# The opening of a recommendation tower on one core: forty gathers in fours that wait for their landing, and a second group of indices spread by products

## What is computed

```python
e = jnp.stack([tbl_0[ids[:, 0]], ..., tbl_39[ids[:, 39]]], axis=1)
z = jnp.einsum('bpd,pde,bpe->bp', e[:, iidx, :], bilinear_matrices, e[:, jidx, :])
h = jnp.concatenate([z, dense_ctx], axis=1)
h = jnp.maximum(h @ W_top1 + b_top1, 0.0)
h = jnp.maximum(h @ W_top2 + b_top2, 0.0)
y = h @ W_top3
```

## Time and profile before

| what | value |
| --- | --- |
| median of 3 runs | 728.96 us (727.7 to 730.28) |
| the profiled execution, its own time | 728.67 us |
| its span, first to last instruction | 726.9 us |
| PE busy | 693.9 us (95%) |
| DVE busy | 597.1 us (82%) |
| POOL busy | 522.2 us (72%) |
| ACT busy | 197.1 us (27%) |
| granted TensorE clock, mean | 0.998 of full speed |
| gathers issued | 416, mean 986 ns |
| pauses | 208, mean 537 ns |

### The profile page before, as it was taken

One profiled execution on the slowest core, in us unless ns is written; L12 is line 12 of the kernel. 1 busy time (PEld: TensorE's weight loads), 2 busy tenths in 40 slices (PEclk: granted clock), 3 DMA queues, 4 the chain that ended last, 5 costly groups with the idle time before them and its releaser, 6 DMA issues.

```text
span 726.9 us, 15700 instructions
## 1 busy us (share of the span) xinstructions
PE 693.9 (95%) x6512; PEld 215.8 (30%) x6512; DVE 597.1 (82%) x608; ACT 197.1 (27%) x309; POOL 522.2 (72%) x631
## 2 busy tenths in 40 slices
PE   2767999999999999999999999999999999999998
PEld 2233333332332232322332232322332222222232
DVE  7989999999986989979876998979967878787800
ACT  3344411422052113043142103143143012213102
POOL 7888888888887888888887888888888887830000
PEclk9999999999999999999999999999999999999999
DMA  4555351222004020000004020000001000000000
GB/s 126 111 89 86 60 99 40 58 52 43 12 12 71 12 40 13 11 12 13 12 12 71 12 35 18 11 12 12 12 12 16 12 12 12 12 8 1 1 1 1
DMA packets 62692, 22.77 MB, mean 31 GB/s; under 512 B 46287, under 2 KB 61805, under 8 KB 62621
## 3 DMA queue, kind: packets, MB, share of 16 engines
q1 hardware_dynamic: 49277, 14.86, 8.8%
q0 software_dynamic: 13312, 6.84, 8.2%
q10 hardware_dynamic: 32, 0.07, 0.1%
HBM read 21.65 MB, written 0.07 MB: 30 GB/s over the span
## 4 chain that ended last, share of the span: by engine, by line
PE 89%; DVE 5%; ACT 4%; DMA 1%; issue 1%; ACTq 0%; DVEq 0%
PE U L940 28%; PE bank_z L965 26%; PE misc L992 14%; PE misc L891 10%; PE U L992 4%; PE U L949 3%; DVE ones L792 3%; PE U L914 3%; ACT x_T L645 1%; DMA idx_wide<-idx_rows 1%; DVE prod L828 1%; ACT x_twin L663 1%; PE bank_z L973 0%; DVE tabs L779 0%; ACT x_twin L666 0%
## 5 line engine op out<-in xcount | busy, mean ns | idle before, releaser
L589 POOL DMA_INDIRECT rows<-in_tbl,idx x416 | 410.2, 986 | 121.3 <-issue 63.5
L828 DVE TENSOR_TENSOR prod<-U,x_T 128x1024 f32<-128x1024 f32 x280 | 329.5, 1216 | 56.5 <-PE U L940 53.7
L965 PE MATMUL bank_z<-prod,select 128*32 128x512 f32 x1600 | 213.1, 604 | 0.7 <-ACT z L625 0.7
L940 PE MATMUL U<-x_T,W 32*128 32x512 f32 x1184 | 187.0, 640 | 7.4 <-ACT x_T L636 3.6
L792 DVE TENSOR_SCALAR ones<-idx_wide,row_of 125x2048 bf16<-125x2048 f16 x140 | 119.0, 872 | 7.0 <-ACT idx_wide L691 3.4
L891 PE MATMUL misc<-ones,tabs 125*32 125x512 bf16 x1680 | 108.4, 388 | 7.3 <-DVE ones L792 5.3
L597 POOL MEMSET pause<- 128x448 uint8 x208 | 111.7, 537 | 0.1
L828 DVE TENSOR_TENSOR prod<-U,x_look 128x1024 f32<-128x1024 f32 x80 | 94.3, 1218 | 21.0 <-PE U L940 18.5
L992 PE MATMUL misc<-z,W 128*32 128x512 f32 x728 | 92.0, 592 | 0.0
L940 PEld LDWEIGHTS U<-x_T,W 32*128 32x128 f32 x1184 | 57.8, 183 | 102.9 <-issue 49.4
L636 ACT ACTIVATE x_T<-U 32x512 f32<-32x512 f32 (+2 forms) x48 | 28.3, 591 | 188.8 <-PE U L914 115.0
(11 more groups left out here) (67 smaller groups left out, 284.1 us busy)
## 6 DMA issues: line engine op xcount, KB each, us to landing
rows<-in_tbl,idx POOLq DMA_INDIRECT x416
idx_wide<-idx_rows SPq DMA_DIRECT2D x13, 500.0 KB
W<-in_W_top SPq DMA_DIRECT2D x100, 8.0 KB
W<-_L_rec_bilinear_matrices SPq DMA_DIRECT2D x72, 16.0 KB, 3.2
prod<-in_tbl SPq DMA_DIRECT2D x4, 156.2 KB
W<-in_W_top SPq DMA_DIRECT2D x35, 2.0 KB
W<-_L_rec_bilinear_matrices SPq DMA_DIRECT2D x4, 128.0 KB
W<-in_W_top SPq DMA_DIRECT2D x1, 512.0 KB
```

The lines of the kernel that those rows point to most:

```text
L589: nc.gpsimd.indirect_dma_start(out=rows[:, n % R_SLOTS, t, f, :], out_offset=None, in_=tables[field][:, :], in_offset=bass.IndirectOffsetO ...
L828: last = nc.vector.tensor_tensor(to[:, :, m * N:(m + n) * N].rearrange("p r (m n) -> p r m n", m=n), U[:, at:at + 2, m * N:(m + n) * N].re ...
L940: last = nc.tensor.matmul(U[:, at + r % 2, m * N:(m + 1) * N], W[row, at_W:at_W + P], x_of(o, a)[row, :], start=True, stop=True, skip_grou ...
L965: last = nc.tensor.matmul(bank_z[r * DIM:(r + 1) * DIM, 0:N], sel, prod[:, (2 * g + r // 2) % P_SLOTS, r % 2, m * N:(m + 1) * N], start=(k ...
```

## The change

Two parts.

1. **Gathers.** The first 40 gathers are issued in fours without the pause; after each four, GpSimd waits until all that were begun on the slot of the last one have landed. From the 41st on, the pairs with pauses stand as before.
2. **Opening.** VectorE converts the first block's indices of all 16 looked-up fields first (4 casts for 1), and clears `rows[:, 1:5]` after that. TensorE spreads the indices of group 1 by 16 more products, and ScalarE copies them into `idx_wide[1]`; the read of `idx_wide` for block 0, group 1 leaves SyncE's list. Group 0's table is split between the one-hots (after two of them, not after five), group 1's follows, and the turned indices for memory come four looks later. ScalarE's clearing of `dense`, VectorE's splits of group 3 and ScalarE's `keep_look(0, 1)` move as well.

The constants `HELD, HELD_BURST = 40, 4` stand beside `BURST = 2`. The diff:

```diff
--- before.py
+++ after.py
@@ -322,6 +322,7 @@
 
 
 BURST = 2
+HELD, HELD_BURST = 40, 4
 
 
 U_SLOTS = 3
@@ -525,7 +526,6 @@
             for f in GROUPS[3]:
                 load_tab(sp, 3, f)
             sp.wait_ge(idx_stored, 16)
-            load_wide(0, 1)
             load_W(2)
             for f in GROUPS[2]:
                 load_tab(sp, 2, f)
@@ -592,7 +592,10 @@
                                 ap=idx[:, OFF[o] // P + t, field:field + 1], axis=0),
                         ).then_inc(gathered[n % R_SLOTS], 16)
                         begun[n % R_SLOTS] += 1
-                        if sum(begun) % BURST == 0:
+                        if sum(begun) <= HELD:
+                            if sum(begun) % HELD_BURST == 0:
+                                pool.wait_ge(gathered[n % R_SLOTS], 16 * begun[n % R_SLOTS])
+                        elif sum(begun) % BURST == 0:
                             pauses += 1
                             nc.gpsimd.memset(pause[:], 0).then_inc(paused, 1)
                             pool.wait_ge(paused, pauses)
@@ -690,22 +693,24 @@
             act.wait_ge(wide_full, 1)
             nc.scalar.activation(idx_wide[0][:], U[0:KP, 2:2 + CF, :], ACT.Copy).then_inc(wide_made, 1)
 
-            nc.scalar.activation(dense[:].rearrange("p t r d -> p t (r d)"),
-                                 ident[:].unsqueeze(1).to_broadcast([P, SUBS, P]), ACT.Copy, scale=0.0
-                                 ).then_inc(dense_zeroed, 1)
             split_hi(0)
             split_mid(0)
+            act.wait_ge(wide_full, 2)
+            nc.scalar.activation(idx_wide[1][:], U[0:KP, 2:2 + CF, :], ACT.Copy).then_inc(wide_made, 1)
+            split_hi(1)
+            split_mid(1)
             act.wait_ge(idx_T_full, 1)
             nc.scalar.activation(idx_T, U[0:NL, 0:BATCH // NB, :].rearrange("p b n -> p (b n)"), ACT.Copy
                                  ).then_inc(idx_T_made, 1)
             act.wait_ge(idx_T_made, 1)
             act.dma_start(idx_rows[:, :], idx_T).then_inc(idx_stored, 16)
-            split_hi(1)
-            split_mid(1)
+            nc.scalar.activation(dense[:].rearrange("p t r d -> p t (r d)"),
+                                 ident[:].unsqueeze(1).to_broadcast([P, SUBS, P]), ACT.Copy, scale=0.0
+                                 ).then_inc(dense_zeroed, 1)
             keep_look(0, 0)
             split_hi(3)
+            keep_look(0, 1)
             split_mid(3)
-            keep_look(0, 1)
             split_hi(2)
             for g in range(-2, G + 1):
                 if g == 4:
@@ -748,9 +753,6 @@
             nc.vector.tensor_copy(ident_h[:], ident[:]).then_inc(ident_h_made, 1)
             dve.wait_ge(row_of_made, 1)
             nc.vector.tensor_copy(row_of[:], row_of_i[:]).then_inc(row_of_f_made, 1)
-            nc.vector.memset(rows[:, 1:5], 0.0).then_inc(rows_zeroed, 1)
-
-
             beside = [(LOOKED.index(f), f, n) for f, n in ((36, 4), (0, 1), (24, 1), (2, 2), (16, 1), (9, 1), (34, 1),
                                                            (23, 1), (28, 1), (22, 1), (30, 1), (27, 1))]
 
@@ -760,7 +762,8 @@
                 return last
 
             dve.wait_ge(ids_loaded, 16)
-            to_half(0, ROWS[0] // P, beside[:1]).then_inc(idx_h_made, 1)
+            to_half(0, ROWS[0] // P, beside[:4]).then_inc(idx_h_made, 1)
+            nc.vector.memset(rows[:, 1:5], 0.0).then_inc(rows_zeroed, 1)
             for a in range(0, CHUNKS, 2):
                 zero = nc.vector.memset(W[:, w_col(a, a):w_col(a, a) + P], 0.0)
             zero.then_inc(W_zeroed, 1)
@@ -783,10 +786,10 @@
                 N, fs = ROWS[o], GROUPS[q]
                 n, job = LOOK_PART[(o, q, k)], LOOK_ORDER.index((o, q))
                 if k == 0:
-                    if job == 0:
-                        dve.wait_ge(wide_made, 1)
+                    if job < 2:
+                        dve.wait_ge(wide_made, job + 1)
                     else:
-                        dve.wait_ge(wide_landed[job % 2], 16 * ((job + 1) // 2))
+                        dve.wait_ge(wide_landed[job % 2], 16 * (job // 2))
                 if n >= ONES:
                     dve.wait_ge(ones_used, n - ONES + 1)
                 nc.vector.tensor_scalar(ones[:, n % ONES, 0:len(fs), 0:N], idx_wide[job % 2][:, 0:len(fs), 0:N],
@@ -833,32 +836,31 @@
                 last.then_inc(multiplied, 1)
 
             dve.wait_ge(row_of_f_made, 1)
-            for k in range(ONES):
+            for k in range(2):
                 one_hot(0, 0, k)
+            split_rest(0)
+            one_hot(0, 0, 2)
+            split_low(0)
+            one_hot(0, 0, 3)
+            split_rest(1)
             dve.wait_ge(ids_rest_loaded, 16)
-            to_half(ROWS[0] // P, BATCH // P, beside[:1])
-            to_half(0, BATCH // P, beside[1:]).then_inc(idx_h_rest_made, 1)
-            split_rest(0)
-            split_low(0)
-            for k in range(ONES, KC):
+            to_half(ROWS[0] // P, BATCH // P, beside[:4])
+            to_half(0, BATCH // P, beside[4:]).then_inc(idx_h_rest_made, 1)
+            for k in range(4, KC):
                 one_hot(0, 0, k)
-                if k == ONES + 1:
-                    split_rest(1)
-                if k == ONES + 3:
+                if k == 5:
                     split_low(1)
             nc.vector.memset(select[:], 0.0).then_inc(select_zeroed, 1)
             nc.vector.memset(rows[:, 5:7], 0.0).then_inc(rows_zeroed, 1)
             for k in range(KC):
                 one_hot(0, 1, k)
-                if k == ONES:
-                    split_rest(3)
-                if k == ONES + 2:
-                    split_low(3)
+            split_rest(3)
             dve.wait_ge(select_zeroed, 1)
             for s in range(CF):
                 at = CF * (UPT - 1) + s
                 last = nc.vector.memset(select[s * DIM:(s + 1) * DIM, at:at + 1], 1.0)
             last.then_inc(constants, 1)
+            split_low(3)
             for n in HOT_AT[-2]:
                 one_hot(*LOOK_OF_PART[n])
             split_rest(2)
@@ -999,21 +1001,25 @@
             pe.wait_ge(ident_h_made, 1)
             pe.wait_ge(idx_h_made, 1)
 
-            for s in range(CF):
-                for t in range(ROWS[0] // P):
-                    last = nc.tensor.matmul(U[0:KP, 2 + s, t * P:(t + 1) * P],
-                                            idx_h[:, t, s:s + 1].to_broadcast([P, KP]), ident_h[:],
-                                            start=True, stop=True, skip_group_check=True)
-            last.then_inc(wide_full, 1)
-            for t in range(BATCH // P):
-                if t == 0:
-                    pe.wait_ge(idx_h_rest_made, 1)
+            for q in (0, 1):
+                if q:
                     pe.wait_ge(wide_made, 1)
-                last = nc.tensor.matmul(U[0:NL, t // SUBS, t % SUBS * P:(t % SUBS + 1) * P], idx_h[:, t, :], ident_h[:],
-                                        start=True, stop=True, skip_group_check=True)
-            last.then_inc(idx_T_full, 1)
+                for s in range(CF):
+                    for t in range(ROWS[0] // P):
+                        last = nc.tensor.matmul(U[0:KP, 2 + s, t * P:(t + 1) * P],
+                                                idx_h[:, t, CF * q + s:CF * q + s + 1].to_broadcast([P, KP]), ident_h[:],
+                                                start=True, stop=True, skip_group_check=True)
+                last.then_inc(wide_full, 1)
             for q in (0, 1):
                 for k in range(KC):
+                    if (q, k) == (0, 4):
+                        pe.wait_ge(idx_h_rest_made, 1)
+                        pe.wait_ge(wide_made, 2)
+                        for t in range(BATCH // P):
+                            last = nc.tensor.matmul(U[0:NL, t // SUBS, t % SUBS * P:(t % SUBS + 1) * P],
+                                                    idx_h[:, t, :], ident_h[:], start=True, stop=True,
+                                                    skip_group_check=True)
+                        last.then_inc(idx_T_full, 1)
                     look(0, q, k)
             pe.wait_ge(constants, 1)
             pe.wait_ge(idx_T_made, 1)
```

## The result

| what | before | after |
| --- | --- | --- |
| median | 729.62 us (4 runs, 727.70 to 731.48) | 739.38 us (4 runs, 733.61 to 739.62) |
| ratio, with 95% interval | | 1.0102 [1.0073, 1.0132] |
| profiled execution: span | 726.9 us | 737.6 us |
| gather 41 starts | 69.97 us | 92.16 us |
| last gather is issued from | 642.70 us | 662.77 us |

The change is slower: 1.0% by the ratio, while the medians lie 9.8 us (1.3%) and the profiled spans 10.7 us apart. The forecast had the sign and the mechanism, with 731.4 us and a range to 736.5: the time lies outside it.

A forecast was written before the change was run, and what follows sets the result against it. TensorE, 95% busy, bounds the kernel, with GpSimd's gather chain 9.65 us ahead behind it. A chain delay of 12.1 less 9.65 adds 2.45 to 728.67, plus 0.29 for the median: 731.4 us, range 725.5 to 736.5.

The forecast's parts named there:

- margin of 9.65 us: End of GpSimd's chain: DMA engines fall silent at 644.80, TensorE turns the last gather's slot at 654.45.
- Nothing could win back a delay: GpSimd between gathers 41 and 416: no wait there can be shortened, so a delay stays to the end.
- the larger of minus the gain and D - 9.65: Whole kernel: change in time is the larger of minus the opening's gain and chain delay beyond margin; + 2.45 us.
- D: Delay of GpSimd's gather chain from the landing waits: 10 L - 10.9, forecast 12.1 us, bounds 0.6 to 17.1.
- The landing L = 2.3 us: First 40 gathers: landing of each four's last gather after its issue ends; seven at 2.8, three at 1.15 us.
- The quiet end: Low bound of the landing: DMA engines silent 1.15 us after the last gather's issue, without other traffic.
- The "high" end: High bound of the landing in the busy opening: 2.8 us after issue, from a 16 KB pair matrix load.
- The gather at 1.10 us: GpSimd's first 40 gathers: each taken at 1.10 us, from 43.98 us over 40 and a sliver.
- So that holds: Turn after gather 40, at 88.45: the forty are in by 81.8, TensorE some 2 us earlier; no harm.
- The opening: Start of the kernel: first multiplication on VectorE at 47.6 for 49.70, a gain of 2.1 us, bounds 0 and 3.5.
- The thin cover of the next indices: Opening's index reads: group 3 at 37.2, needed 38.0; group 2 at 50.1, needed 50.0; lateness cuts the gain.
- Slower: Late-chain case: GpSimd's delay over 11.85 us, time up by 2.2 to 7.45 us; chance 0.48.

The follow-up runs named there:

- gathers_only: Kernel before with only the new gather loop (first 40 gathers in fours waiting for their landing), old opening: 1.0108 of before, 739.21 us.
- opening_only: "The opening alone": changed kernel with its new opening, but every gather in pairs with pauses as before: 0.9948 of before, 726.97 us.
- held_20: Changed kernel with the landing waits stopped at gather 20 instead of 40: 0.9953 of before, 727.89 us; 1.0176 on a slower chip.
- small_reads: Changed kernel with each read of indices cut from 512 columns to 32 (looked-up rows not the reference's): 0.9983 of before.
- held_in_quiet: Kernel before with gathers 193 to 232 in fours that wait for their landing, instead of pairs with pauses: 0.9980 of before, 730.24 us.
- fewer_pauses_later: Changed kernel with a pause only after every fourth gather, not every second, behind the first 40: 0.9978 of before, 731.15 us.
- pause_in_fours: Changed kernel with the first 40 gathers in fours, each ended by the pause instead of a landing wait: 0.9949 of before, 727.32 us.

## Why the prediction was wrong

- **What bounds the kernel** (TensorE, and behind it a GpSimd chain with a margin of 9.65 us): right. "Nothing could win back a delay" was so within the spread of executions: of 22.2 us at gather 41, 20.1 were left at the last gather (662.77 - 642.70), and the chain from gather 41 on took 572.7 us before, 570.6 after, and 569.0 to 569.7 in others.
- **The sum's form** (the larger of minus the gain and D - 9.65): right. 20.1 - 9.65 = 10.4 against 10.7 us measured in the spans, and `gathers_only` gives the same time with the old opening. Taken from the opening alone (last gather at 640.35, margin 9.6, span 724.4), the same form fits every kernel with late waits: 3.8 us worked out for 4.2 measured in `held_20`, 5.3 for 5.8 in `small_reads`, 12.9 for 13.2 in the change, 13.2 for 13.5 in `gathers_only`.
- **The landing L = 2.3 us: the term that failed.** Ten waits sum to 32.4 us; less the gap of 0.27 each that is 2.97 for L. Where I put seven fours at 2.8 and three at 1.15, the trace has seven of 2.8 to 5.7 and three of 1.65 to 1.94, gap included. The quiet end was right but for 0.3 us (1.15 was counted to the silence of the DMA engines, and in `held_in_quiet` GpSimd goes on 1.33 us after the issue at the earliest). The "high" end was not an upper bound: it was the landing of direct loads of 16 KB, taken 8 to 12 us into the kernel, and a gather beside heavier traffic takes longer (5.66 us at 103 GB/s, 4.82 at 132). "Hardly all ten" was true, and the mean of the ten lay above it all the same. This is 6.7 of the 10.1 us by which D was short.
- **The gather at 1.10 us: a smaller miss.** The stretch table for the gathers of the first 92 us:

```profile
0.00:92.00 92.00, 47.36 (x40) 0.93 0.44 90
```

47.36 / 40 = 1.18 for 1.10; 3.4 us. The longest, 2.26 and 2.53 us, stand from 12 to 21 us, beside VectorE's splits of groups 0 and 1, which the new opening has put there; with the old opening (`gathers_only`) the forty took 44.98 us, 1.12 each. With these two, 3.21 + 47.36 + 30 x 0.305 + 32.4 = 92.1, the measured start of gather 41. At D = 20.1 in place of 12.1 my own sum gives 728.67 + 10.4 + 0.29 = 739.4.
- **"So that holds", of the turn after gather 40: wrong**, for the same reason. It waited 6.96 us, and it wasn't "the first turn that could suffer" either: the turn after gather 20 had waited 1.81. They did not add to the end, since the chain was later still; without that, `fewer_pauses_later` shows, the early waits cost some 5 us, a term that the sum lacked. Only by luck the "about 4.5 us" of idle time forecast for the last turns was met (4.67): the early waits had taken up the rest of the delay.
- **The opening: right in its steps, and nearly in its size.** 2.1 us were worked out, 3.4 show; with pauses, as the steps were counted, 2.6 (`opening_only`). The rest goes with the pauses that are gone, which the forecast had named: the one-hots ran at 0.66 us each in group 1 (6.58 / 10), not 0.77, and in the opening alone the same ten took 7.81. "Late next" was named rightly: the split of group 3 (1.77 us of waiting). The thin cover of the next indices gave way as feared, 2.91 us in the changed kernel, 0.32 with pauses.
- **The chances.** "Slower" at 0.48 was the likeliest case; the range's end of 736.4 rested on the bound for L that was none. Seven waits of `held_in_quiet`, 1.60 to 1.72 us, end, less the gap, 1.33 to 1.45 us after the end of an issue and 2.3 to 2.4 after its start; the opening's end up to 5.4 us after the issue. The fixed cost of some 2.0 us in the Trainium skill (DMA: Bandwidth & Descriptors, anatomy of one DMA on the GpSimd path) agrees in size with the quiet ones counted from the start of the issue, and not with the opening's.

## What to carry to other kernels

An engine that never waits is a bound with a margin, even at 72% busy: measure by how much its last product precedes its use, in more than one trace (9.6 to 12.8 us here), and count every delay of it from the start of the kernel against that margin. Count also each use on the way: a product that is late for an early one can cost by itself (some 5 us in `fewer_pauses_later`). A wait for a landing in a loop of DMA issues costs the landing as it is among the traffic of that moment; read its upper bound from the slowest transfer there, not from one of its own size, and where it is wanted for other reasons, stop it while the margin lasts (20 gathers here, not 40). And two effects on different engines of one chain don't add: test each alone before crediting either.

## What the hardware showed beyond that

- **Pauses hit one-hots.** Over 20 to 85 us the one-hots take (ns min/median/max), with pauses in the opening alone and without any until 94 us in the changed kernel:

```profile
L795 DVE TENSOR_SCALAR ones<-idx_wide,row_of x45: 732/754/1309, 20.4 to 83.9; 125x2048 bf16<-125x2048 f16 x45
```

```profile
L795 DVE TENSOR_SCALAR ones<-idx_wide,row_of x45: 624/744/948, 19.8 to 82.7; 125x2048 bf16<-125x2048 f16 x45
```

In the opening alone all nine one-hots of the first 95 us that take over 1.0 us overlap a pause, and without pauses none takes over 0.99 (`gathers_only`). Five in a row take 3.98 us there and 3.40 in the changed kernel. One of the nine, the longest, and the pause beside it (timelines of DVE and POOL):

```profile
50.04 1.31 DVE L795 TENSOR_SCALAR ones<-idx_wide,row_of 125x2048 bf16<-125x2048 f16 x1
```

```profile
50.31 0.49 POOL L600 MEMSET pause<- 128x448 uint8 x1
```

It takes 0.56 us more than the median, a little over the pause's whole 0.49, though it began 0.27 us before the pause did. The Trainium skill's SBUF — State Buffer (two separate sides) has VectorE, in some of its modes, and GpSimd lock each other out for whole instructions, whichever starts first. The trace agrees in the size; in the order it doesn't, since here the instruction that started first is the one that was held up. The shortest one-hots (624 ns in the changed kernel) are not explained by missing pauses: in `pause_in_fours`, 625 and 1276 stand side by side.
- **Run to run.** Kernels that wait for landings vary with them: the changed kernel has one execution of 733.61 among 739.4, and the ten waits sum to 32.4, 34.2 and 37.3 us in the profiles of three kernels that share them.
